# Moving the spreading of B from TensorE to ScalarE and three products' sums from GpSimd to TensorE, in a scan-plus-experts kernel on one core

## The reference, cut to what matters

```
delta = softplus((x @ Wd.T) @ W_dt.T + b_dt)      # [b, t, 256]
B, C  = 16 values each per row, projections of x
for n in 16 states:
    h[n] = scan over t:  h = exp(delta * A[:, n]) * h + delta * B[n] * x
y     = sum over n of h[n] * C[n]  +  D * x
experts: softmax gate over 8 experts, 128 rows of a batch per expert,
         gelu(rows @ W1 + b1) @ W2 + b2, scaled by the gate, added to those rows
out   = input + y + experts
```

## Time and profile before

| | |
|---|---|
| median of 3 runs | 2436.53 us (2431.91 to 2438.82) |
| the profiled execution's own time | 2436.61 us |
| its span, first to last instruction | 2434.8 us |
| mean granted TensorE clock | 0.985 of full speed |
| busy share of the span | PE 96%, DVE 97%, ACT 80%, POOL 87% |
| DMA | 335.90 MB, 138 GB/s in the mean |

### The profile page before, as it was taken

The page is one execution under the profiler, slowest core; times in us unless marked ns, Lnnn a source line. Parts: engine busy times, 40 slices in busy tenths (PEclk is TensorE's granted clock), DMA queues, the critical chain, the costliest instruction groups (busy, mean ns, idle before and its releaser), DMA issues.

```text
span 2434.8 us, 33569 instructions
## 1 busy us (share of the span) xinstructions
PE 2330.9 (96%) x11004; PEld 1853.9 (76%) x11004; DVE 2355.9 (97%) x2010; ACT 1955.6 (80%) x3374; POOL 2126.1 (87%) x1204
## 2 busy tenths in 40 slices
PE   7849999999999999999999999999999999999996
PEld 4437778877877788778777877788778778777885
DVE  6799999999999999999999999999999999999996
ACT  7747888888888888888888888888888888888873
POOL 4427999999999899999999999999999989999996
PEclk9969999999999999999999999999999999999998
DMA  9957464535444444444545353444545354454433
GB/s 345 345 174 243 131 189 130 151 96 138 116 120 140 118 129 113 135 118 101 156 105 152 94 146 102 117 134 124 137 110 139 104 139 114 108 150 103 99 100 52
DMA packets 120926, 335.90 MB, mean 138 GB/s; under 512 B 17488, under 2 KB 69808, under 8 KB 104112
## 3 DMA queue, kind: packets, MB, share of 16 engines
q1 hardware_dynamic: 65776, 249.60, 29.1%
q0 software_dynamic: 53760, 83.92, 20.2%
q10 hardware_dynamic: 1216, 0.23, 0.0%
HBM read 256.61 MB, written 91.75 MB: 143 GB/s over the span
## 4 chain that ended last, share of the span: by engine, by line
PE 86%; issue 4%; DVE 3%; DMA 2%; ACT 2%; POOL 1%; SPq 1%; ACTq 0%; POOLq 0%; DVEq 0%
PE bank_l L1188 35%; PE bank_l L1123 35%; PE bank_b L1076 4%; PE bank_t L1069 4%; PE bank_t L1043 3%; PE bank_t L1052 2%; PE bank_l L1184 2%; PE bank_t L1060 1%; DMA xn_rows<-c_all 1%; ACT og L732 1%; DVE hid L825 1%; DVE hid L823 1%; DVE prod L826 1%; POOL ysum L570 1%; DVE bank_x L909 0%
## 5 line engine op out<-in xcount | busy, mean ns | idle before, releaser
L570 POOL TENSOR_TENSOR ysum<-ysum,prod 128x1024 f32<-128x1024 f32 x416 | 1098.0, 2639 | 43.2 <-DVE prod L981 38.0
L970 DVE TENSOR_TENSOR_SCAN bank_x<-decay,bank_x 128x1024 f32<-128x1024 f32 x448 | 1024.5, 2287 | 20.8 <-ACT decay L698 11.8
L1123 PE MATMUL bank_l<-ext,w_sb 128*128 128x256 f32 x4096 | 980.0, 382 | 27.7 <-ACT og L732 24.7
L1188 PE MATMUL bank_l<-w_sb,hid 128*128 128x256 f32 x4096 | 952.6, 383 | 0.0
L1123 PEld LDWEIGHTS bank_l<-ext,w_sb 128*128 128x128 f32 x4096 | 761.6, 191 | 178.8 <-ACT og L732 32.9
L1188 PEld LDWEIGHTS bank_l<-w_sb,hid 128*128 128x128 f32 x4096 | 762.6, 190 | 161.2 <-issue 52.5
L707 ACT ACTIVATE hid<-bank_l,b_all 128x256 f32<-128x256 f32 x1024 | 429.8, 471 | 374.0 <-PE bank_l L1123 373.6
L698 ACT ACTIVATE decay<-delta,a_sb 128x511 f32<-128x511 f32 x1024 | 640.1, 707 | 1.2
L909 DVE TENSOR_TENSOR bank_x<-du,bank_b 128x1024 f32<-128x1024 f32 x512 | 616.8, 1205 | 0.1
L981 DVE TENSOR_TENSOR prod<-bank_x,c_all 128x1024 f32<-128x1024 f32 x448 | 544.7, 1216 | 0.1
L525 POOL DMA_INDIRECT out<-og,idx_all x256 | 410.3, 1603 | 43.8 <-POOL ysum L570 42.7
(11 more groups left out here) (105 smaller groups left out, 1919.9 us busy)
## 6 DMA issues: line engine op xcount, KB each, us to landing
c_all<-bc_rows SPq DMA_DIRECT2D x128, 1024.0 KB, 5.2
w_sb<-in_w SPq DMA_DIRECT2D x32, 1024.0 KB, 10.7
decay<-in_x SPq DMA_DIRECT2D x32, 512.0 KB, 7.0
xn_rows<-c_all SPq DMA_DIRECT2D x32, 512.0 KB, 6.5
out<-yrow POOLq DMA_DIRECT2D x32, 512.0 KB, 6.4
xr<-xn_rows SPq DMA_DIRECT2D x30, 512.0 KB, 6.4
bc_rows<-prod SPq DMA_DIRECT2D x32, 192.0 KB, 5.1
rank<-bc_rows SPq DMA_DIRECT2D x32, 128.0 KB, 5.4
```

What stands on the lines that cost most here:

```text
L570: nc.gpsimd.tensor_tensor(ysum[:, m % 2], first, prod[:, i], ALU.add).then_inc(sum_done, 1)
L970: nc.vector.tensor_tensor_scan(into, decay[:, k % 2, i].rearrange("p c t -> p (c t)"), bank_x[:, s % 2], 0.0, ALU.mult, ALU.add).then_inc( ...
L1123: i = nc.tensor.matmul(bank_l[(q + v) % 2][:, (f % 2) * UT:(f % 2 + 1) * UT], w1_sb[:, e2, hc, f * P:(f + 1) * P], ext[:, v % 2, hc], star ...
L1188: i = nc.tensor.matmul(o, hid[:, w % 2, f, c * K:(c + 1) * K], w2_sb[:, w_par, f], start=False, stop=(f == FC - 1 and c == UB - 1))
```

## The change

TensorE spreads B only for the steps with n % 4 == 0; for the others (`WIDE`) SyncE loads one row of B broadcast to 128 partitions into b_wide, and ScalarE copies it to bank_b. The products of steps 1, 11, 13 and 15 are made by GpSimd; those of 11, 13 and 15 stay in kept (one buffer of three) and are added by TensorE when it turns y, as is D * x, by a matmul of xnt with a diagonal matrix of D. skip and state go, xnt gets four buffers and yrow one, blocks of y are contiguous in time, and the small jobs change places.

```diff
-GP_STEPS = (4, 12)
-KEPT = 4
+GP_STEPS = (1, 11, 13, 15)
+KEPT = (11, 13, 15)
+SUMS = tuple(n for n in range(1, N) if n not in KEPT)
+SLOTTED = tuple(n for n in range(N) if n not in KEPT + GP_STEPS)
+WIDE = (1, 2, 3)
-        out_tiles = out.rearrange("b (p c) d -> b p c d", p=P)
+        out_tiles = out.rearrange("b (c p) d -> b p c d", p=P)
...
+            def load_b_wide(u, i):
+                held(b_ready, (u - 1) * STEPS + WIDE[i] + 1)
+                row = R + u % SLOTS * STEPS + WIDE[i]
+                sp.dma_start(b_wide[:, i:i + 1], bc_rows[u // SLOTS:u // SLOTS + 1, row:row + 1, :]
+                             .broadcast_to([P, 1, T])).then_inc(bw_in[i], 16)
...
-                pool.dma_start(out_tiles[y], yrow[:, y % 2], accum_op=ALU.add).then_inc(y_added, 16)
+                pool.dma_start(out_tiles[y], yrow[:], accum_op=ALU.add).then_inc(y_added, 16)
...
+                                tile = kept[:, KEPT.index(n)] if n in KEPT else zabs[:]
+                                nc.gpsimd.tensor_tensor(tile, tile, c_all[:, u % 2, i][:, None, :].broadcast_to([P, HC, T]),
                                                         ALU.mult).then_inc(gp_prod_done, 1)
...
-                        if i == 3 and sl == 0 and there(b - 2, NB) and u < NU:
-                            add_y(b - 2, u)
-                        if i == 3 and sl == 2 and b == NB - 1:
+                        if i == 3 and sl == (3 if b < NB - 1 else 2) and 0 < b < NB:
                             add_y(b - 1, u)
...
                 act.wait_ge(y_tr, y * 2 + half + 1)
...
+                wait(act, y_added, y * 16)
+                nc.scalar.copy(yrow[:, 2 * half:2 * half + 2], bank_t[:].rearrange("p (c d) -> p c d", c=2)).then_inc(yrow_done, 1)
...
                 wait(act, delta_done, nb - 1)
+                wait(act, sum_done, sums((nb - 2) * N + 2) if nb > 1 else 0)
...
-            def skip_term(par, loaded, used):
...
+            def spread_b(s):
+                act.wait_ge(bw_in[s % STEPS - WIDE[0]], (s // STEPS + 1) * 16)
+                act.wait_ge(bx_done, s)
+                nc.scalar.copy(bank_b[:], b_wide[:, s % STEPS - WIDE[0]]).then_inc(b_ready, 1)
...
                     for pair in range(FC // 2):
+                        if there(u, NU) and pair in (0, 2):
+                            spread_b(u * STEPS + 1 + pair // 2)
                         if there(v, NU):
                             gelus(v, v, pair)
-                        if pair == 0 and sl == 2 and there(b, NB) and there(b + 1, NB):
-                            take_z(b + 2, (m + 1) % 2, 1)
-                        if pair == 0 and 0 < b < NB and sl == y_slot(b):
-                            take_yrow(0, b - 1)
-                        if pair == 0 and sl < HC and there(b, NB) and there(b + 2, NB):
-                            take_xr(b + 2, m % 2, sl)
+                        if pair == 0 and sl == 0 and there(b, NB) and there(b + 2, NB):
+                            take_xr(b + 2, 1)
+                        if pair == 0 and sl == 1 and there(b, NB) and there(b + 1, NB):
+                            take_z(b + 2, (m + 1) % 2, 0)
+                        if pair == 0 and sl == 2 and 0 < b < NB:
+                            take_yrow(1, b - 1)
+                        if pair == 0 and sl == 3 and there(b + 3, NB):
+                            take_xr(b + 3, 0)
...
+                    if there(u, NU) and 3 in WIDE:
+                        spread_b(u * STEPS + 3)
...
-                            take_z(b + 2, (m + 1) % 2, 0)
-                    if 0 < b < NB and sl == y_slot(b):
-                        take_yrow(1, b - 1)
-                    if sl == 3 and there(b, NB) and there(b + 1, NB):
-                        skip_term((m + 1) % 2, (j * 2 + (m + 1) // 2 + 1) * 16, b * 2)
+                            take_z(b + 2, (m + 1) % 2, 1)
+                    if sl == 0 and 0 < b < NB:
+                        take_yrow(0, b - 1)
...
+                        if n in KEPT:
+                            wait(dve, y_tr, b * 2)
...
+                        if n in KEPT:
+                            to = kept[:, KEPT.index(n)]
+                        else:
+                            wait(dve, sum_done, read(b, n))
+                            to = prod[:, slot(n)]
...
-                        for term in (ysum, kept, skip):
-                            o = nc.tensor.matmul(part, term[:, par, dt, :].rearrange("p (r c) -> p c r", c=TC)[:, c], ident[:],
-                                                 start=(term is ysum), stop=(term is skip), is_transpose=True)
+                        rows = slice(c * P, (c + 1) * P)
+                        nc.tensor.matmul(part, ysum[:, y % 2, dt, rows], ident[:], start=True, stop=False, is_transpose=True)
+                        for n in range(len(KEPT)):
+                            nc.tensor.matmul(part, kept[:, n, dt, rows], ident[:], start=False, stop=False, is_transpose=True)
+                        o = nc.tensor.matmul(part, xnt[:, y % 4, dt, rows], diag[:, dt], start=False, stop=True)
...
-                            if q % 2 == 0 and there(s + 1, NB * N):
+                            if q % 2 == 0 and (n + 1) % STEPS not in WIDE and there(s + 1, NB * N):
...
+                        if q == 1 and there(b, NB):
+                            if sl == 0 and there(b + 2, NB):
...
+                                turn_rows(b + 2, 1)
+                            if sl == 1 and there(b + 1, NB):
+                                wait(pe, yrow_done, b * 2 - 1)
+                                expand(b + 2, 0)
+                            if sl == 2 and b > 0:
...
+                                y_rows(b - 1, 1)
+                            if sl == 3 and there(b + 3, NB):
+                                turn_rows(b + 3, 0)
...
+                            if sl == 0 and 0 < b < NB:
+                                y_rows(b - 1, 0)
+                            if sl == 1 and there(b, NB) and there(b + 1, NB):
+                                expand(b + 2, 1)
```

More of the change, by code:

```diff
@@ L221, in build @@
         picks_done = sem("picks_done")
-        xnt_in = [sem(f"xnt_in{i}") for i in range(2)]
+        xnt_in = [sem(f"xnt_in{i}") for i in range(4)]
         xr_in = sem("xr_in")
@@ L266, in sums, with slot, read @@
         def sums(s):
-            return s - (s + N - 1) // N - (s + N - 1 - KEPT) // N
+            return s // N * len(SUMS) + sum(n < s % N for n in SUMS)
+        def slot(n):
+            return SLOTTED.index(n) % 4
+        def read(b, n):
+            q, r = divmod(b * len(SLOTTED) + SLOTTED.index(n) - 4, len(SLOTTED))
+            return sums(q * N + max(SLOTTED[r], 1) + 1)
         def gp_prods(s):
@@ L400, in _ @@
             load_c(0)
+            held(logits_done, NB)
+            for i in range(len(WIDE)):
+                load_b_wide(0, i)
             for g in range(2, NG):
@@ L660, in take_yrow @@
                 act.wait_ge(y_tr, y * 2 + half + 1)
-                if y == 0 and half == 0:
-                    for g in range(2):
-                        act.wait_ge(parts_out[g], NG // 2 * 48)
-                wait(act, y_added, (y - 1) * 16)
-                nc.scalar.copy(yrow[:, y % 2, 2 * half:2 * half + 2], bank_t[:].rearrange("p (c d) -> p c d", c=2)).then_inc(yrow_done, 1)
+                wait(act, y_added, y * 16)
+                nc.scalar.copy(yrow[:, 2 * half:2 * half + 2], bank_t[:].rearrange("p (c d) -> p c d", c=2)).then_inc(yrow_done, 1)
             def take_z(nb, par, dt):
@@ L739, in _ @@
             act.wait_ge(logits_done, NB)
-            skip_term(0, 16, 0)
             for dt in range(HC):
@@ L961, in main @@
                         dve.wait_ge(bx_done, s + 1)
[L962 to L964 removed]
+                        if s == KEPT[0]:
+                            for g in range(2):
+                                dve.wait_ge(parts_out[g], NG // 2 * 48)
+                        if n in KEPT:
+                            wait(dve, y_tr, b * 2)
+                        if n in GP_STEPS and n in KEPT:
+                            into = kept[:, KEPT.index(n)].rearrange("p c t -> p (c t)")
                         elif n in GP_STEPS:
[L966 to L967 removed]
+                            dve.wait_ge(delta_done, b + 1)
+                            into = zabs[:].rearrange("p c t -> p (c t)")
                         else:
@@ L1061, in turn_rows, with y_rows @@
                 o.then_inc(xr_tr, 1)
-            def y_rows(par, half):
+            def y_rows(y, half):
+                if half == 0:
+                    pe.wait_ge(sum_done, sums(y * N + N))
+                    pe.wait_ge(gp_prod_done, gp_prods(y * N + N))
+                    pe.wait_ge(prod_done, dve_prods(y * N + N))
+                    pe.wait_ge(xnt_in[y % 4], (y // 4 + 1) * 16)
+                    pe.wait_ge(diag_made, HC)
                 for c in (2 * half, 2 * half + 1):
@@ new lines, in main @@
```

(9 more changed lines are left out.)

119 lines of the change are left out of this document (42 added, 77 removed).

## The result

| | median us | range, runs | against before |
|---|---|---|---|
| before | 2437.43 | 2431.91 to 2438.82, 4 | 1 |
| after | 2618.76 | 2615.40 to 2625.99, 4 | 1.0752 [1.0723, 1.0782] |
| forecast | 2477 | 2402 to 2512 | 1.017 |

The change makes the kernel 7.5% slower. "Slower" was forecast, by 1.7%, and the time lies outside the stated range: 142 us are missing from the sum.

What follows compares the result with a forecast made beforehand. TensorE and VectorE were taken as equally full, with ScalarE's arrival at `scale_og` deciding. Laps and 0.2 us for bank_b gave 71.05 against 69.84 us; 31 x 1.2 + 3 = +40 on 2436.6: 2477 us, range 2402 to 2512.

Steps and rivals of the forecast that it cites:

- A and B: Laps of a batch between ends of the fourth `up`, sl 2 to 3 and 3 to 0: 17.25 and 17.0 us.
- C and D: Laps of a batch between ends of the fourth `up`, sl 0 to 1 and 1 to 2: 18.2 and 18.4 us.
- rival 1: Faster: waits for `scale_og` do not bind, TensorE's work decides; 2388 us, at best 2362; chance 0.25.
- `take_yrow` a unit behind `add_y`: Single yrow buffer: ScalarE's next write comes a unit after GpSimd issues the transfer; no cost charged.
- the bound of 4.4 us: GpSimd's `add_y` with four times the pieces: from nothing to 4.4 us more; taken as 0.
- the term for the diagonal: TensorE's matmul for D * x in y: 0.108 us for 128 columns, taken from the ordinary 256-column matmul.
- the spread behind the fourth `up`: TensorE, each unit: removing this spread of B saves 0.31 us, the other spreads 0.22 each.
- the 0.2 us charged for bank_b: TensorE's spread for step 4 waits for the second `multiply_b` to end, some 0.2 us.
- the rows' transfers: SyncE's loads of B rows, 256 KB each, 384 in all: issued a whole unit (17 us) before needed.
- Rival 3: Slower by more: ScalarE's copy waits for `multiply_b` and holds the gelus, or `add_y` takes 4.4 us; 2520 us, chance 0.13.
- Rival 2: No change: waits for `scale_og` half as long because copies are short (0.2 us); 2432 to 2450 us, chance 0.12.
- The signs I had named: Spreads x128, 384 copies into bank_b, 64 `scale_og` waits, VectorE idle some 3.5 us a batch, ysum transposes 0.108 apart.

Runs made afterwards that it cites:

- e1: The changed kernel with `add_y` issued one unit earlier, in sl = 2 and not sl = 3: 2532.49 us, 1.0394 of the kernel before.
- e4: e1 with all 16 spreads of B on TensorE again, no b_wide and no copies of it on ScalarE: 2515.83 us, 1.0327 of the kernel before.
- e2: The changed kernel with the output's old layout, 4 KB pieces and blocks read with a step of four: 2596.21 us, 1.0652 of the kernel before.
- e5: e1 with x in place of D * x in y, the diagonal replaced by the identity: 2505.18 us, 1.0281 of the kernel before.
- e3: The kernel before with only the output's new layout, 1 KB pieces and contiguous blocks: 2435.33 us, 0.9989 of the kernel before.

## Why the prediction was right or wrong

**Right: the direction and its mechanism.** The small jobs that padded A and B moved to C and D, TensorE then reaches the second `up` before ScalarE has done `scale_og`, and the batch grows although both full engines have less to do. A 17.25 and B 17.0 were forecast, 17.35 and 17.09 measured; 64 waits for `scale_og` forecast, 61 in e1. Without the failed step below the kernel is still 3.9% slower (e1), so the direction was not luck, though the sum was short for it too. "The waits for `scale_og` do not bind" (rival 1) is refuted by the same rows. That the copies neither win nor lose in the steady part is e4 against e1: 72.27 and 72.22 us a batch.

**Wrong, 1: "`take_yrow` a unit behind `add_y`", at no cost.** This is the step that failed. I named the single buffer and priced it at nothing, because I took "a unit" for a distance and set no landing time against it. The distance from GpSimd's issue to ScalarE's copy is 9.0 us, because GpSimd reaches `add_y` late in its unit and `take_yrow` stands before the end of the next; the landing took 12.6 us. Cost 86 us by e1. The profile's list of issues had a landing of 6.4 us, but even 6.4 against 9.0 would have said that nobody waits: it was measured with 4 KB pieces, at a place with little company. e1 and e2 each take the wait away, so it needed both the near place and the longer landing, and the longer landing came of the small pieces and the other transfers together (the table in e2). The layout's four times as many pieces I had priced only on GpSimd's issue, where it cost 0.45 us; the bound of 4.4 us was far too wide there, and on the landing there was no bound at all.

**Wrong, 2: the term for the diagonal**, 0.108 us, from eight instructions of 256 columns in 1.73 us. The eight instructions are four matmuls: the 32-bit matmuls of `up` and of the diagonal appear twice in the trace, the transposes once (4 transposes for `turn_rows`, x4; 4 matmuls for `up`, x8). So 128 columns cost 0.22. Mis-sized by 0.91 us a batch, 27 us by e5.

**Wrong, 3: the spread behind the fourth `up`** was charged with 0.31 us; 0.09 of it is there without it (the `up` of 1228.56 ends 1.73 later, the next instruction starts at 1230.38 in the changed kernel). That is 0.36 us a batch, against which the 0.2 us charged for bank_b did not come: in e1 the spread waits 4 times, 2.0 us in all. With 0.1 us of other small differences it makes the 0.26 us a batch that the diagonal leaves of e1's 1.17, 8 us.

**Wrong, 4: the rows' transfers**, "a whole unit (17 us) before it is needed". In the steady part nobody waits for them in e1; in the first three batches they cost 16 us, by e4 against e1. They also lengthened the landing of `add_y`: 9.2 us without them, 10.7 with them (e4, e1).

**Small slips in the sums.** B adds up to 17.07 and not 17.0, and the rows of B are 100.7 MB in the profile's count and not 98. Nothing hangs on either.

The sum: 2477 + 86 + 27 + 8 + 16 = 2614 against 2619. The rest, 5 us, I can't place, and no run was made for it. The 8 us come from the sums of the laps; no run took them apart.

**The rivals.** Rival 3 named "ScalarE's copy waits and holds the gelus" and "`add_y` takes its 4.4 us" on GpSimd, 2520: GpSimd had slack (82% busy), and its issue took 1.9 us. The wait was ScalarE's, but behind a transfer, not behind `multiply_b`. Rival 2 needed short copies: one takes 0.60 us into PSUM, and the next instruction starts 0.52 after it (1204.57 to 1205.09), where I had charged 0.48; copies from PSUM take 0.59. The Trainium skill's ScalarE: Activation LUTs, "Step-by-step: what each stage is for", has the rule that I cited, that ScalarE is faster into PSUM than into SBUF. These rows show no gain of it, but the two kinds of copy differ in their source as well, so they don't test it, and no run shows the 0.1 us that I took from it. GpSimd's issue went from 1.45 to 1.9 us for four times the pieces. The Trainium skill's DMA: Bandwidth & Descriptors, "Anatomy of one DMA", says that many descriptors can be given out before their number costs; the trace agrees in that the cost is small, 0.45 us. That row says nothing of when they have landed, which was the point.

**The signs I had named:** spreads x128, copies x384 and transposes 0.11 apart are there; VectorE waits for ScalarE's copies 4.4 us a batch in e1 (3.5 forecast).

## What to carry to other kernels

When a change removes a buffer, work out the distance in time between the issue of the transfer and the next write to the buffer, with the places at which both engines really stand, and set it against a landing time that fits the new pieces and the transfers that will stand beside it; "it is a unit later" is no number, and a landing measured at another place (6.4 us here) can be half of what comes (12.6). Where three or four engines are within 2% of each other, the order on the in-order engine that serves the others (here ScalarE's tail before `scale_og`) sets the time: cut the loop into laps at one repeating instruction, and sum each lap for each engine. Count how often an operation appears in the trace against how often the code issues it, before its duration is divided.

## What the runs showed of the hardware that I had not expected

- A 512 KB accumulating transfer landed 6.4 us after its issue in 4 KB pieces and 6.9 in 1 KB pieces while the other queues moved 12 to 56 GB/s (before, e3), and 9.4 and 12.6 us while they moved 146 to 192 (e2, after).
- A 32-bit matmul of 128 columns is two instructions, 0.23 us from start to next start; a 32-bit transpose of the same size one, 0.11. Read with a step of four elements, the first takes 0.45 us, the second 0.12.
- Copies of 128 x 512 by ScalarE took 0.60 us from SBUF into PSUM and 0.59 out of it (L740 and L682 of the changed kernel).
